# Two selective-scan layers: GpSimd's rows shifted by 8 bytes, side work moved to other steps, one logarithm for three units

## The chip, the cores and the metric

One Trainium2 chip, one of its cores. The metric is device time in microseconds for the whole program, one launch; the median of three runs of the kernel before is 16709.1 us (16696.06 to 16725.33). The engines are named by the profile's short names: PE (TensorE), DVE (VectorE), ACT (ScalarE), POOL (GpSimd), SP (SyncE).

## The reference

Four residual layers over x of shape (4, 96, 56, 56), each `x = x + L(groupnorm(x))`. Layer 0 is attention, layer 2 a local top-k attention with a feed-forward part; the change doesn't touch them. Layers 1 and 3 are state-space layers. Their scans, over 192 channels, 16 states and every position of the image in 8 (layer 1) or 4 (layer 3) orders, are what is changed.

Layer 1, per order:

```python
hc = hc * jnp.exp(d_t[..., None] * A[None]) + (d_t * u_t)[..., None] * B_t[:, :, None, :]
y_t = jnp.einsum('bkdn,bkn->bkd', hc, C_t)
```

Layer 3, per order:

```python
dlt = jax.nn.softplus(dlt)
phi = jnp.exp(-jnp.cumsum(dlt[..., None] * A_log[None, :, :, None, :], axis=3))
dbx = dlt[..., None] * jnp.swapaxes(b, 2, 3)[:, :, None] * xs[..., None]
h = phi * jnp.cumsum(dbx / (phi + 1e-12), axis=3)
y = jnp.einsum('bkdln,bknl->bkdl', h, c) + Ds[None, :, :, None]
```

In both, the step `dlt` is a softplus of a projection of the input, and B and C are rows of another projection of it.

## The kernel before, in words

`scans` handles one layer for one pair of images: two images of 192 channels make three blocks of 128 partitions, the **units** c = 0, 1, 2. It is called four times, twice with `ratio` false (layer 1) and twice with `ratio` true (layer 3). A **tile** q is 448 positions (T) of one order: 8 x 7 = 56 tiles a call in layer 1 (layer 1's image rows are 64 wide in memory, and half its orders are diagonals, whose pieces are cut in two), 4 x 7 = 28 in layer 3. A tile has 16 **groups**, one for each state n; the group's number over the whole call is g, r is its place in the tile, u = 3g + c counts group and unit. The **step** is s = 3r + c, 0 to 47 in a tile.

Main work of one group:
- ACT, `decay` (L1200): exp(dl x A) for each unit. Layer 1 has a ring of two in PSUM (NA = 2), so `decay(u)` waits for scan u - 2; layer 3 a ring of six in SBUF. In layer 3 ACT also does `weight` (L1210, a Tanh) into a ring of three in PSUM (NW = 3), where weight(u) waits for scan u - 3. `seed` (L1233) puts the start value at a row's head.
- POOL, `input1` (L1415): Tr = du x B for all three units at once, 128 x 1344, two groups ahead.
- DVE, `scan` (L1333), the recurrence over 449 elements (the start value and 448), one for each unit. Before it, in layer 3, `input2` (L1315) multiplies Tr with the weight. The state goes to PSUM for c < ON_DVE (two units in layer 1, one in layer 3) and else to `Hr` in SBUF.
- DVE `project` (L1340) and POOL `project` (L1424): Hc = state x C, the first for the states in PSUM and the second for those in `Hr` (one row of 448 in layer 1, two in layer 3). DVE does its projections between the scans of units 1 and 2.
- ACT, `keep_psum` (L1216) and `keep_sbuf` (L1221): the last column of each state into `st`, the start value for the next tile. A scan into PSUM waits for `st_done` of the group before, since it overwrites the state there.
- PE, `gather_n` (L1079): adds Hc into y in PSUM by a product with the identity.

Side work makes the next tile's `xs`, `dl`, `du` and (layer 3) `cs` while this tile runs, one tile ahead, at steps that tables fix (`SIDE`, `MERGE`, `AFTER`, and `prepare`/`prepare_late` of PE): ACT `gather` xs (L1114), PE `proj` (L1030), ACT `keep_dts` (L1126) and `keep_rows` (L1120), PE `pre_delta` (L1035), ACT `absolute` (L1133), `positive` (L1137), `expo` (L1142), in layer 1 `one_plus` and `minus_w`, ACT `loga` (L1158), PE `total` (L1043 to L1047, a sum by four products with the identity), ACT `delta` (L1162), then DVE `inputs` (L1283, du) in layer 1, and DVE `cumsum` (L1299) and POOL `inputs` (L1400, du) in layer 3. In layer 3 DVE `one_less` (L1290) makes w1. `merge` (L1191) writes the last tile's y back. In layer 3 the logarithm needs another table than Tanh and Exp, so that two table loads stand around it.

Every engine works its instructions in the order of the program; semaphores alone hold them. The loop of ACT, for each u: weight(u + 2) in layer 3, decay(u + 2), at c = 0 `seed`, at c = 2 `keep_sbuf`, then merge and side work of the step, and then at c = 1 `keep_psum`. `dl` and `du` have rows of 448 elements, `Hr` rows of 449, all packed without gaps.

## Time and profile before

| | us |
|---|---|
| median of 3 runs | 16709.1 |
| profiled execution, its own time | 16707.5 |
| its span | 16705.6 |
| DVE busy | 14926.7 (89%) |
| PE busy | 13571.3 (81%) |
| POOL busy | 12620.4 (76%) |
| ACT busy | 12298.3 (74%) |
| scans of layer 1, first call, 2350 to 6122 | 3771.1 |
| scans of layer 3, first call, 11001 to 13496 | 2494.4 |

A row of groups reads: line, engine, operation, tiles written and read with partitions x elements, count, then total busy us and mean ns of one, then the idle time just before them and what ended it. Times in windows and timelines are us from the span's start.

### The profile page before, as it was taken

Reading aid. Unit: us, or ns where it says so; the run is one execution under the profiler, and the core shown is the slowest. Engines: PE = TensorE matmul, PEld = TensorE weight load, DVE = VectorE, ACT = ScalarE, POOL = GpSimd, SP = SyncE. Lnnn points to the kernel's source line nnn. Section 1 sums busy time; section 2 is a strip of 40 time slices with the busy share of each in tenths; the row PEclk is TensorE's granted clock in tenths of the full one; section 3 lists DMA queues with packets and bytes.
Section 4 is the critical chain, followed back from the end, with each engine's and each line's share of the span. In section 5 each row is a group of like instructions: output and inputs, shape, how many; then the busy total and the mean of one; then the engine's idle time right before and its main releaser. Section 6 shows DMA issues by size and latency. Waiting matters only on the chain. (4 is left out here: it accounts for less than half of the span.)

```text
span 16705.6 us, 189354 instructions
## 1 busy us (share of the span) xinstructions
PE 13571.3 (81%) x38048; PEld 5620.9 (34%) x38048; DVE 14926.7 (89%) x20527; ACT 12298.3 (74%) x27189; POOL 12620.4 (76%) x6313
## 2 busy tenths in 40 slices
PE   7988978888888878888888886877777777777777
PEld 2222223333333333333333333533333333333333
DVE  6666669999999988999999996889999988999998
ACT  3555567777777766777777774588888968888996
POOL 0000059999999978999999994289999968999996
PEclk9999989999999999999999998988888888888988
DMA  1100023333333333333333332122222212222221
GB/s 24 19 14 17 5 74 113 112 113 112 111 111 111 111 96 107 112 113 113 111 111 111 111 111 80 49 78 85 85 84 83 84 48 80 85 85 84 83 84 46
DMA packets 543207, 1404.94 MB, mean 84 GB/s; under 512 B 135566, under 2 KB 191926, under 8 KB 539430
## 3 DMA queue, kind: packets, MB, share of 16 engines
q1 hardware_dynamic: 542034, 1392.84, 29.0%
q14 instruction: 868, 7.11, 0.2%
q8 instruction: 305, 5.00, 0.1%
HBM read 1311.24 MB, written 58.30 MB: 82 GB/s over the span
## 5 line engine op out<-in xcount | busy, mean ns | idle before, releaser
L1415 POOL TENSOR_TENSOR Tr<-du,BC 128x1344 f32<-128x1344 f32 x2688 | 8174.7, 3041 | 138.5 <-DVE du L1283 137.2
L1079 PE MATMUL PS<-Hc,ident 128*128 128x448 f32 x16128 | 7115.6, 578 | 1363.7 <-POOL Hc L1424 1133.9
L1079 PEld LDWEIGHTS PS<-Hc,ident 128*128 128x128 f32 x16128 | 3063.8, 199 | 5308.9 <-issue 2706.6
L1200 ACT ACTIVATE PS<-dl,A 128x448 f32<-128x448 f32 x5376 | 3401.9, 633 | 1599.8 <-DVE Hr L1333 1054.9
L1424 POOL TENSOR_TENSOR Hc<-Hr,BC 128x448 f32<-128x448 f32 (+1 forms) x2688 | 3603.9, 1341 | 602.2 <-DVE Hr L1333 527.1
L1333 DVE TENSOR_TENSOR_SCAN PS<-PS,Tr 128x449 f32<-128x449 f32 x3584 | 3711.0, 1078 | 93.0 <-ACT st L1216 82.4
L1340 DVE TENSOR_TENSOR Hc<-PS,BC 128x448 f32<-128x448 f32 x4480 | 2568.9, 607 | 0.0
L1210 ACT ACTIVATE PS<-cs,lneps,A 128x448 f32<-128x448 f32 x2688 | 1935.1, 720 | 18.8 <-DVE PS L1333 1.0
L1333 DVE TENSOR_TENSOR_SCAN Hr<-PS,Tr 128x449 f32<-128x449 f32 x1792 | 1938.4, 1082 | 0.0
L1333 DVE TENSOR_TENSOR_SCAN Hr<-Ar,PS 128x449 f32<-128x449 f32 x1792 | 1931.7, 1078 | 0.0
L1315 DVE SCALAR_TENSOR_TENSOR PS<-PS,Tr 128x448 f32<-128x448 f32 x2688 | 1651.1, 614 | 223.2 <-ACT PS L1210 203.6
L1200 ACT ACTIVATE Ar<-dl,A 128x448 f32<-128x448 f32 x2688 | 1765.8, 657 | 0.0
L486 DVE TENSOR_REDUCE mx<-PS 128x1 f32<-128x448 f32 (+1 forms) x2100 | 1207.9, 619 | 574.4 <-PE PS L276 559.2
L678 POOL MEMSET pad<- 128x348 f32 x6 | 2.3, 389 | 2217.9 <-POOLq L67 2217.9
L435 ACT ACTIVATE Pr<-PS 128x896 f32<-128x896 f32 (+1 forms) x1092 | 953.7, 887 | 668.3 <-PE PS L339 664.8
L1333 DVE TENSOR_TENSOR_SCAN PS<-Ar,PS 128x449 f32<-128x449 f32 x896 | 972.2, 1085 | 0.0
L1216 ACT ACTIVATE st<-PS 128x2 f32<-128x2 f32 (+1 forms) x2688 | 447.5, 166 | 637.9 <-DVE Hc L1340 635.5
L276 PE MATMUL PS<-K,Q 96*128 96x448 bf16 (+1 forms) x2100 | 800.3, 388 | 89.5 <-DVE mx L486 56.0
L1090 PE MATMUL PS<-yacc,ident 128*128 128x448 f32 (+15 forms) x1320 | 771.3, 693 | 84.8 <-ACT yacc L1191 82.1
L1035 PE MATMUL PS<-dts,dw 12*128 12x448 f32 x1008 | 522.9, 600 | 325.5 <-ACT dl L1137 203.8
L339 PE MATMUL PS<-Q,K 99*128 99x448 bf16 (+1 forms) x2100 | 748.9, 370 | 7.7 <-ACT Q L404 3.6
L1043 PE MATMUL PS<-du,ident 128*128 128x448 f32 x1008 | 517.4, 597 | 261.0 <-DVE cs L1299 177.2
(271 smaller groups left out, 15394.8 us busy)
## 6 DMA issues: line engine op xcount, KB each, us to landing
BC<-bcscratch SPq DMA_DIRECT2D x5376, 224.0 KB, 3.6
zscratch<-zst SPq DMA_DIRECT2D x84, 224.0 KB, 1.9
bcscratch<-rows SPq DMA_DIRECT2D x336, 56.0 KB, 1.7
z<-zscratch SPq DMA_DIRECT2D x28, 672.0 KB, 4.8
xg<-mid SPq DMA_DIRECT2D x12, 1176.0 KB, 7.9
xr<-mid SPq DMA_DIRECT2D x56, 168.0 KB, 2.7
rl<-rows SPq DMA_DIRECT2D x56, 168.0 KB, 3.3
Q<-part SPq DMA_DIRECT2D x72, 98.0 KB, 4.4
```

The source lines that it names most:

```text
L276: e.matmul(PS[0:qn, 5 + n % 2, 0:T], Q[s][0:96, q0:q0 + qn], KK[s][0:96, i * T:i * T + T], start=True, stop=True).then_inc(mx_mm, 1)
L435: e.activation(Pr[0:kn, n % NPR, 0:nt, :], PS[0:kn, 2 * (n % 2):2 * (n % 2) + nt, 0:T], ACT.Exp, scale=scale).then_inc(s_exp, 1)
L486: e.tensor_reduce(mx[0:qn, t, i:i + 1], PS[0:qn, 5 + n % 2, 0:T], AX.X, ALU.max).then_inc(mx_red, 1)
L1079: e.matmul(PS[:, YB + c, 0:T], K["ident"][:], Hc[:, g % NHC, c, :], start=False, stop=(nn == 15)).then_inc(y_done, 1)
L1090: e.matmul(view(PS[:, YB + c, :], ro, rd), K["ident"][:], view(yacc, c * n + off, dims), start=(i == 0), stop=False)
L1200: e.activation(decay_at(u, 1), dl[:, q % 2, c, :], ACT.Exp, scale=A[:, q // NT, c, nn:nn + 1]).then_inc(a_done, 1)
L1210: e.activation(PS[:, u % NW, 1:TW], cs[:, q % 2, c, :], ACT.Tanh, scale=A2[:, q // NT, c, nn:nn + 1], bias=K["lneps"][:]).then_inc(w_done, 1)
L1315: e.scalar_tensor_tensor(out=p, in0=p, scalar=1.0, in1=Tr[:, g % NTR, c, :], op0=ALU.add, op1=ALU.mult).then_inc(t2_done, 1)
L1333: e.tensor_tensor_scan(state_at(g, c, 0), decay_at(u, 0), input_at(g, c), 1.0 if ratio else 0.0, ALU.mult, ALU.add).then_inc(s_done, 1)
L1340: e.tensor_tensor(Hc[:, g % NHC, c, :], state_at(g, c, 1), BC[:, g % NBS, 1, :], ALU.mult).then_inc(h_done, 1)
L1415: e.tensor_tensor(Tr[:, g % NTR] if ratio else Tr[:, g % NTR, :, 1:TW], du[:, q % 2], b, ALU.mult).then_inc(t_done, 1)
L1424: e.tensor_tensor(Hc[:, g % NHC, ON_DVE:3], Hr[:, g % NH, :, 1:TW], c_, ALU.mult).then_inc(hp_done, 1)
```

## The change

Three things, all in `scans`.

1. `dl`, `du` and `Hr` get rows with a pitch of 452 elements (1808 bytes) and an offset of two elements, so that the rows that POOL reads, `dl` and `du` from their first element and `Hr` from its second, begin 8 bytes behind a multiple of 16. `BC`, `xs`, `Tr` and `Hc` stay as they are.
2. Steps of the side work move. Layer 3: third gather 8 to 10, dts and rows 10, 11 to 13, 14, the nine softplus steps from 13..23 to 16..28, logarithm 25 to 29, deltas 32, 36, 41 to 34, 38, 42, DVE's `one_less` 26 to 30, cumsums 33, 37, 42 to 35, 39, 43, PE's `proj`, `pre_delta` one group later, all three `total` behind `gather_n`. Layer 1: the third delta 41 to 40, and ACT's `keep_psum` goes ahead of merge and side work of its step. `total` takes `dl` and `du` first and waits for `minus` and `logd` only ahead of the products that need them.
3. In layer 3 one `Ln` over 128 x 1344 takes the place of three over 128 x 448.

```diff
-    TW = T + 1
+    TW, TP = T + 1, T + 4
...
-        xs, dl, du = sb("xs", [128, 3, T]), sb("dl", [128, 2, 3, T]), sb("du", [128, 2, 3, T])
+        xs = sb("xs", [128, 3, T])
+        dl, du = (sb(i, [128, 2, 3, TP])[:, :, :, 2:2 + T] for i in ("dl", "du"))
...
-        Hr = sb("Hr", [128, NH, 3 - ON_DVE, TW])
+        Hr = sb("Hr", [128, NH, 3 - ON_DVE, TP])[:, :, :, 1:1 + TW]
...
-                e.wait_ge(minus, q + 1 if ratio else 3 * q + c + 1)
                 if c and q:
                     e.wait_ge(total_read, 3 * q + c)
-                e.matmul(X_, K["ident"][:], du[:, s, c, :], start=True, stop=False)
+                e.wait_ge(expd, 3 * q + c + 1)
+                e.matmul(X_, K["ident"][:], dl[:, s, c, :], start=True, stop=False)
+                e.matmul(X_, K["ident"][:], du[:, s, c, :], start=False, stop=False)
+                e.wait_ge(minus, q + 1 if ratio else 3 * q + c + 1)
                 e.matmul(X_, K["nident" if ratio else "ident"][:], w1[:, c, :], start=False, stop=False)
                 e.wait_ge(logd, 3 * q + c + 1)
-                e.matmul(X_, K["ident"][:], logs(q)[:, c, :], start=False, stop=False)
-                e.matmul(X_, K["ident"][:], dl[:, s, c, :], start=False, stop=True).then_inc(x_full, 1)
+                e.matmul(X_, K["ident"][:], logs(q)[:, c, :], start=False, stop=True).then_inc(x_full, 1)
 
             def prepare(q, r):
-                if r == 3:
+                first = 4 if ratio else 3
+                if r == first:
                     proj(q)
-                elif r in (4, 5):
-                    pre_delta(q, r - 4)
+                elif r in (first + 1, first + 2):
+                    pre_delta(q, r - first - 1)
                 elif r == 6 and not ratio:
                     pre_delta(q, 2)
-                elif r == (10 if ratio else 9):
+                elif r == 9 and not ratio:
                     total(q, 0)
-                elif r == 11 and ratio:
-                    total(q, 1)
 
             def prepare_late(q, r):
-                if r == 6 and ratio:
+                if ratio and r == 7:
                     pre_delta(q, 2)
-                elif r == 10 and not ratio:
-                    total(q, 1)
-                elif r == 12:
-                    total(q, 2)
+                elif ratio and 10 <= r < 13:
+                    total(q, r - 10)
+                elif not ratio and r in (10, 12):
+                    total(q, r // 2 - 4)
...
             def logs_together(q, i):
-                for c in range(3):
-                    loga(q, c)
+                e.wait_ge(expd, 3 * q + 3)
+                if q:
+                    e.wait_ge(cs_ready, 3 * q)
+                e.activation(logs(q)[:], du[:, q % 2], ACT.Ln, bias=K["one"][:]).then_inc(logd, 3)
...
             if ratio:
-                SIDE = {gather: (5, 7, 8), rows_or_dts: (10, 11), absolute: (13, 17, 21), positive: (14, 18, 22),
-                        expo: (16, 20, 23), logs_together: (25,), delta: (32, 36, 41)}
+                SIDE = {gather: (5, 7, 10), rows_or_dts: (13, 14), absolute: (16, 20, 25), positive: (17, 22, 26),
+                        expo: (19, 23, 28), logs_together: (29,), delta: (34, 38, 42)}
             else:
                 SIDE = {gather: (4, 6, 7), rows_or_dts: (10, 11), absolute: (13, 16, 19), positive: (14, 17, 20),
                         expo: (15, 18, 21), one_plus: (22, 23, 25), minus_w: (24, 27, 30), loga: (26, 28, 31),
-                        delta: (29, 35, 41)}
+                        delta: (29, 35, 40)}
...
                 if c == 2:
                     keep_sbuf(g)
+                if c == 1 and not ratio:
+                    keep_psum(g)
                 if q and s in MERGE:
                     merge(q - 1, MERGE.index(s))
                 if q + 1 < NQS:
                     prepare(q + 1, s)
-                if c == 1:
+                if c == 1 and ratio:
                     keep_psum(g)
...
-                if ratio and s == 26:
+                if ratio and s == 30:
                     one_less(q)
...
-            AFTER = (33, 37, 42) if ratio else (31, 37, 42)
+            AFTER = (35, 39, 43) if ratio else (31, 37, 42)
```

## Rows read from the trace of the kernel before

**Rows 1.** The page: busy times; one group with what ended its idle time.

```profile
PE 13571.3 (81%) x38048; PEld 5620.9 (34%) x38048; DVE 14926.7 (89%) x20527; ACT 12298.3 (74%) x27189; POOL 12620.4 (76%) x6313
...
L1424 POOL TENSOR_TENSOR Hc<-Hr,BC 128x448 f32<-128x448 f32 (+1 forms) x2688 | 3603.9, 1341 | 602.2 <-DVE Hr L1333 527.1
```

**Rows 2.** Windows, first scan stage of each layer: length, busy by engine, clock, DMA.

```profile
core 0: us, PE busy (x) PEld busy (x) DVE busy (x) ACT busy (x) POOL busy (x), PEclk, DMA share, GB/s
2350.40:6121.50 3771.10, 3243.55 (x7832) 1402.07 (x7832) 3706.97 (x4635) 2833.68 (x7110) 3584.84 (x1786) 0.99 0.38 111
...
11001.00:13495.40 2494.40, 1848.26 (x3814) 768.01 (x3814) 2380.47 (x3231) 2221.20 (x4685) 2290.91 (x972) 0.89 0.29 83
```

**Rows 3.** DVE's waits, layer 1, 2350 to 6122: us, times, longest.

```profile
DVE PS L1333 <- ACT st L1216: 40.3, 112, 0.9
DVE du L1283 <- ACT dl L1162: 18.1, 55, 0.6
```

**Rows 4.** DVE's waits, layer 3, 11001 to 13496.

```profile
DVE PS L1315 <- ACT PS L1210: 101.6, 69, 2.7
```

**Rows 5.** Timelines of DVE and ACT, layer 1, a diagonal tile's steps 4 to 6.

```profile
5715.55 2.08 DVE L1333 TENSOR_TENSOR_SCAN PS<-PS,Tr 128x449 f32<-128x449 f32 x2 [0.38 <-ACT st L1216]
...
5714.26 1.10 ACT L1114 ACTIVATE xs<-xc 128x264 f32<-128x264 f32 x2
```

**Rows 6.** Timeline of POOL, layer 1, groups 3 and 4: start, us.

```profile
2357.05 1.13 POOL L1424 TENSOR_TENSOR Hc<-Hr,BC 128x448 f32<-128x448 f32 x1
...
2361.12 0.98 POOL L1424 TENSOR_TENSOR Hc<-Hr,BC 128x448 f32<-128x448 f32 x1
```

**Rows 7.** Groups by form, whole span.

```profile
L1415 POOL TENSOR_TENSOR Tr<-du,BC 128x1344 f32<-128x1344 f32 x2688 | 8174.7, 3041 | 138.5 <-DVE du L1283 137.2 <-PE PS L1079 1.1
...
L1400 POOL TENSOR_TENSOR du<-dl,xs 128x448 f32<-128x448 f32 x168 | 190.8, 1136 | 77.9 <-ACT dl L1162 73.1 <-PE PS L1079 4.8
...
L2377 ACT ACTIVATE E<-S,nb 112x616 f32<-112x616 f32 x40 | 32.3, 808 | 49.7 <-DVE nb L2502 49.7
...
L2377 ACT ACTIVATE E<-S,nb 112x315 f32<-112x315 f32 x16 | 8.9, 557 | 20.7 <-DVE nb L2502 20.5
```

**Rows 8.** Timeline of POOL, layer 3: L1424 during L1290, and the next.

```profile
11921.55 2.46 POOL L1424 TENSOR_TENSOR Hc<-Hr,BC 128x896 f32<-128x896 f32 x1 [0.42 <-DVE Hr L1333]
...
11930.16 1.92 POOL L1424 TENSOR_TENSOR Hc<-Hr,BC 128x896 f32<-128x896 f32 x1 [3.15 <-DVE Hr L1333]
```

**Rows 9.** Timelines of DVE and ACT, layer 1, a tile's steps 41 and 42.

```profile
3064.27 1.08 DVE L1333 TENSOR_TENSOR_SCAN Hr<-PS,Tr 128x449 f32<-128x449 f32 x1
...
3066.67 0.62 DVE L1283 TENSOR_TENSOR du<-PS,xs 128x448 f32<-128x448 f32 x1 [0.32 <-ACT dl L1162]
...
3065.45 0.64 ACT L1200 ACTIVATE PS<-dl,A 128x448 f32<-128x448 f32 x1 [0.89 <-DVE Hr L1333]
```

**Rows 10.** Timelines of DVE and ACT, layer 3, a tile's steps 25 to 28.

```profile
11921.39 0.83 DVE L1290 TENSOR_SCALAR w<-du 128x1344 f32<-128x1344 f32 x1
11924.91 0.63 DVE L1315 SCALAR_TENSOR_TENSOR PS<-PS,Tr 128x448 f32<-128x448 f32 x1 [2.68 <-ACT PS L1210]
...
11919.70 1.28 ACT L1158 ACT_TABLE_LOAD   x1
11920.99 1.79 ACT L1158 ACTIVATE cs<-du,one 128x448 f32<-128x448 f32 x3
```

**Rows 11.** Timelines of PE, ACT, DVE around step 10 in layer 3; one window there.

```profile
11979.51 4.17 PE L1030 MATMUL PS<-xs,xp 128*76 128x448 f32 x6 [1.97 <-ACT xs L1114]
...
11983.78 0.54 ACT L1126 ACTIVATE dts<-PS 12x448 f32<-12x448 f32 x1 [1.80 <-PE PS L1030]
...
11985.15 0.63 DVE L1315 SCALAR_TENSOR_TENSOR PS<-PS,Tr 128x448 f32<-128x448 f32 x1 [1.34 <-ACT PS L1210]
...
11980.00:11983.40 3.40, 3.40 (x6) 1.25 (x5) 3.40 (x6) 1.98 (x5) 3.40 (x2) 0.50 0.30 76
```

**Rows 12.** Timeline of PE, layer 3: first and last products of a sum.

```profile
11937.84 0.99 PE L1043 MATMUL PS<-du,ident 128*128 128x448 f32 x2 [2.37 <-DVE cs L1299]
...
11941.29 1.48 PE L1047 MATMUL PS<-dl,ident 128*128 128x448 f32 x2
```

More of the change, by code:

```diff
@@ L1155, in loga @@
                 e.wait_ge(expd, 3 * q + c + 1)
-                if ratio and q:
-                    e.wait_ge(cs_ready, 3 * q)
                 e.activation(logs(q)[:, c, :], du[:, q % 2, c, :], ACT.Ln, bias=K["one"][:]).then_inc(logd, 1)
@@ L1244, in act @@
                 positive(0, c)
-            for step in (expo, loga) if ratio else (expo, one_plus, minus_w, loga):
+            for step in (expo,) if ratio else (expo, one_plus, minus_w, loga):
                 for c in range(3):
                     step(0, c)
+            if ratio:
+                logs_together(0, 0)
             for c in range(3):
```

## The prediction

> **What bounds the kernel now.** I read four views in this order: busy times of the page, windows over the four scan stages, VectorE's own waits there, and the timeline around each wait.
>
> The page gives VectorE (DVE) 89% of the span, ScalarE (ACT) 74%, GpSimd (POOL) 76% [rows 1]. The change touches only the scans, and a stage of these takes 3771.1 us in layer 1 and 2494.4 us in layer 3 [rows 2]. Each layer has two such stages of one and the same code, for two pairs of images; I take the second as the first, 12.53 of 16.71 ms in all. In them VectorE is busy 98% (3706.97 of 3771.10) and 95% (2380.47 of 2494.40), GpSimd 95% and 92%. Both look like the bound, so the waits decide. In layer 1 VectorE waits for GpSimd in no row that is listed: 40.3 us in 112 waits for ScalarE's `st` (L1216), 18.1 us in 55 for its `dl` (L1162) [rows 3]. In layer 3 it waits 101.6 us in 69 waits for ScalarE's weights (L1210) [rows 4]. GpSimd in turn waits for VectorE: 527.1 us for L1333 ahead of its L1424 [rows 1]. So VectorE is the bound, with a few holes that ScalarE makes, and GpSimd follows it. VectorE's instructions overlap by about 0.09 us when nothing holds them (two scans of 1.08 take 2.08 together [rows 5]), so a hole costs its idle time plus 0.09.
>
> **Part 1: the starts of the rows.** In layer 1 GpSimd's L1424 takes 1.13 us for group 3 and 0.98 for group 4, and so on in threes: 1.13, 0.98, 0.98 [rows 6]. Its operand `Hr` has a pitch of 449 elements: its three slots begin 4, 8 and 12 bytes behind a multiple of 16 (the program places tiles at multiples of 32 bytes), and BC at 0. The long one is the first slot, so offsets 0 to 4 are slow and 8 to 12 fast. L1400, both operands at 0, takes 1136 ns: slow too [rows 7]. One row of 448 at 1131 and three at 3041 (L1415) give 955 per row and 176 fixed; the fast 978 gives 802 per row. In layer 3 L1424 reads a slow and a fast row: 176 + 955 + 802 = 1933, measured 1.92 where nothing disturbs it [rows 8]. The model holds, and behind the change every row lies at 8. L1415: 3041 to 176 + 3 x 802 = 2582, 2688 times, 1234 us. L1424: 0.15 on a third of 1792, 90 us; 0.153 on 896, 137 us. L1400: 0.153 x 168, 26 us. GpSimd loses 1487 us of work. On the path that is worth about nothing: no hole of VectorE ends with GpSimd. I take 3 us, for the first L1415s of each stage that VectorE has to await (two of them, 0.46 each, in four stages), and keep 0 to 10. ScalarE, VectorE and TensorE read and write these rows as well. No row has ScalarE read `dl` at 8 (L1200), and I take no difference (bounds -5 to +5 ns on 2 x 2688 + 2688 instructions beside slack, zero on the path).
>
> The Trainium skill (GPSIMD Engine Reference, Elementwise — side-by-side cycle accounting) calls about 2.6 cycles per element the floor of a two-input operation, whatever the start; by it the shift would bring GpSimd nothing. At the 1.2 GHz that the page gives, that is an estimated 2.17 ns per element; the fast rows run at 802/448 = 1.79 ns, so the trace speaks against it, and as GpSimd isn't the bound the time would be the same either way.
>
> **Part 2: layer 1, `keep_psum` ahead of the side work.** At steps s = 1, 4, 7 ScalarE first does a merge or a gather, then L1216, and the scan of the next group waits for `st`. One such hole is 0.38, behind a gather of 1.10 [rows 5]. Now L1216 goes first: it waits only for VectorE's second L1340, then takes 0.17, with a whole scan (1.0) of cover. Behind it on ScalarE wait the side work and the next decay L1200. That decay couldn't start before the following scan ends anyway (it starts 0.10 behind it [rows 9]); it is due 0.9 after that end and takes 0.64. From the second L1340's end, L1216 leaves at 0.3, side work of up to 0.98 (start to start) at 1.25, the decay may start at 1.1 and must start by 1.3: everything fits, except s = 7 on diagonal tiles, where the gather of s = 6 already ran late: there 0.16 is left over, on 28 of 56 tiles of a stage (4.5 us). The 112 holes cost 40.3 + 112 x 0.09 = 50.4 us a stage. **Delta** of the third unit moves from s = 41 to 40: L1283 now waits 0.32 for it [rows 9]; at 40 it starts behind L1216 with the sums of TensorE complete, and is done before it is due. 18.1 + 55 x 0.09 = 23.0 us. Layer 1: 2 x (50.4 + 23.0 - 4.5) = 138 us. If only the half came: 69; if no residue stayed: 147.
>
> **Part 3: layer 3.** Holes of a stage by step, from the timeline of VectorE (overlap included): 27 at the logarithms, 2.68 idle + 0.09 [rows 10], 75 us; 27 of 0.23 just ahead, 6; 13 at s = 11 and 12, 20; 14 at s = 9 of 0.65, 9; s = 3 and 6 on transposed tiles, 9. Together 119.
> *Logarithms.* Three L1158 take 1.79 us with two table loads of 1.28 around [rows 10]. One over 1344 columns: the slope from 315 to 616 columns is (808 - 557)/301 = 0.834 ns [rows 7], so 0.654 + 896 x 0.000834 = 1.40; 0.39 less. But it moves from s = 25 (c = 1) to 29 (c = 2), and so behind `keep_sbuf`, which waits for the scan of c = 2. Count from the start of the c = 1 scan: keep_sbuf ends at 3.44, load to 4.73, Ln to 6.14, load to 7.43, weight to 8.16; VectorE is due at 5.30 (scans, L1315, L1290). Hole 2.9, as now: 24.91 - 22.13 = 2.78. Gain of the shorter Ln: nothing. The 0.23 ahead goes, since ScalarE's side work there is no longer on four steps in a row (20 to 23). Together 81 to 77: 4 us.
> *L1290* reads `du`, now three rows with gaps. It takes 834 ns for 1344 elements, and while it runs GpSimd's L1424 took 2.46 for 1.92 [rows 8]. The Trainium skill (VectorE: DVE Perf Modes, Mode 2×_2P) asks that the outermost counts of source and destination be both even or odd and equal. By it, with `w` still one run of 1344 against three rows, the double rate is lost. Bounds from rows: 834 to 3 x 0.61 = 1830. Either way it lies within the 2.9 us in which VectorE awaits the weight: 0 on the path, and up to 1.0 x 54 = 54 us if that cover were gone. I keep 0.
> *Steps 11, 12.* L1126 waits 1.80 for the six L1030 records of 4.17 us, in a stretch with TensorE's granted clock at 0.50, its lower level of 1.2 GHz, behind a wait of its own of 1.97 us for the third gather at s = 8; VectorE then idles 1.34 [rows 11]. Now the third gather is at 10 and L1126 at 13, three steps for two: 1.7 us more room, more than the 1.34. 20 us go to 2.
> *Step 9.* The gather of s = 8 leaves: 9 to 2 us. Steps 3 and 6 stay.
> *What is late next:* cumsums at 35, 39, 43 and deltas at 34, 38, 42: the sum of the third unit has three steps for four. From cumsum to delta I count 5.2 us; the sum's eight records took 4.9 in a stretch where the clock fell to its lower level (records of 1.48 for two instead of 0.99) [rows 12]: it fits. GpSimd's L1400 waits a unit longer; it then has 2.6 + 1.8 + 1.0 us of work until the next tile's first product and 1.9 us in hand.
> Layer 3: 2 x (4 + 18 + 7) = 58; I take off 4 a stage for holes at the new places: 50 us.
>
> **Sum.** 16707.5 (the profiled execution; its span is 16705.6, the median 16709.1, so no correction) - 138 - 50 - 3 = 16516; forecast **16518 us**, 1.1% less.
>
> **Rivals.**
> *A. The logarithm brings its saving:* if ScalarE reached it as early as today, 0.39 x 54 = 21, and the new places cost nothing (8), no residue (9): 16480. For it: ScalarE has more idle steps ahead of s = 29. Against: keep_sbuf stands in front.
> *B. In layer 1 the wait moves to the decay.* Twelve of 16 c = 1 steps have side work, now all behind L1216. If the decay came 0.08 late on each: 12 x 0.08 x 112 = 108 us back: 16626. It decides from side work over 1.0 us, or if L1216 starts more than 0.1 behind L1340. For it: the margin at gathers is only 0.05 to 0.2; against: nine of the twelve are single instructions on 448 columns, of the kind of L1162 and L1158 (a third of 1.79 us [rows 10]), with half a us of room.
> *C. Slower: TensorE late at the end of layer 3's tiles.* The third sum starts behind the cumsum of s = 39 instead of 37. If TensorE then carries the backlog of L1079 over the tile's end at half clock, merges and L1340 (ring of three) wait. Two steps are 3.4 us; 54 x 3.4 = 184 plus layer 3's lost gain of 50: 16752. It decides once TensorE still has over two groups waiting at s = 45. Against: TensorE is busy 1848 of 2494 us [rows 2], so it has room, and GpSimd's product, which it waits for, comes earlier now.
> *D. GpSimd's saving reaches the end:* only if VectorE's holes were GpSimd's. Its ceiling is all holes but the logarithms': 147 + 88 + 3: 16470; joined with A's 21, 16449.
>
> **How the numbers follow.** Forecast (16490 to 16560) 62%; A and D together 14%; B, full or in part (16560 to 16640), 17%; C in full 3%; C in part, or an offset that makes ScalarE or VectorE slower (16640 to 16740) 4%. Range 16450 to 16640. About 0.2% (33 us) is what a measurement of this kernel tells from no change. Faster by more than that 0.93, within it 0.04, slower 0.03.
>
> **What would show it.** L1415 at 2.58 and L1424 at 0.98 in all slots and 1.78 in layer 3; no wait of VectorE for L1216 or L1162 in layer 1, its busy share there near 99.8%; scans of 3702 and 2470 us; the hole at the logarithms still 2.7 to 2.9, now behind L1290; no wait of L1126. Wrong it would be if L1200 appears among VectorE's waits, if L1333 or L1200 last longer, or if TensorE appears behind L1340.

## The result, and the profile after

The kernel after takes 16480.4 us (median of 4 runs, 16477.67 to 16489.0); the kernel before, measured beside it, 16712.8 us (4 runs, 16696.06 to 16725.33). The ratio is 0.9862 with a 95% interval of [0.9845, 0.988]: 232 us, 1.4% less. The forecast was 16518 us, 38 us above the result and within its range.

The profiled execution has a span of 16478.4 us, 227.2 less than the 16705.6 of before. First the page: busy time, share of the span and instructions of each engine.

```profile
PE 13585.7 (82%) x38048; PEld 5582.2 (34%) x38048; DVE 14909.9 (90%) x20527; ACT 12365.2 (75%) x27077; POOL 11077.5 (67%) x6313
```

GpSimd lost 1543 us of work, 9% of the span, and the span fell by 1.4%: most of GpSimd's saving went into its own waiting. Second, the windows over the first scan stage of each layer, which answer to [rows 2]. The windows of [rows 2] lie 11 us behind the scans that they are meant for: the first scan of layer 1 starts at 2339.3, that of layer 3 at 10990.0. The lengths are right; from first scan to last VectorE was busy 3710.22 us and GpSimd 3594.92 in layer 1, 2386.12 and 2299.88 in layer 3.

```profile
core 0: us, PE busy (x) PEld busy (x) DVE busy (x) ACT busy (x) POOL busy (x), PEclk, DMA share, GB/s
2342.00:6034.50 3692.50, 3247.99 (x7844) 1406.62 (x7844) 3691.01 (x4645) 2872.74 (x7120) 3135.26 (x1790) 0.99 0.40 113
10832.70:13294.00 2461.30, 1858.61 (x3820) 750.61 (x3821) 2397.43 (x3243) 2226.91 (x4648) 1990.04 (x975) 0.90 0.30 85
```

| scan stage, us | before | after | less | forecast |
|---|---|---|---|---|
| layer 1, first and second call | 3771.1, 3771.6 | 3692.5, 3695.4 | 154.8 | 138 |
| layer 3, first and second call | 2494.4, 2495.4 | 2461.3, 2460.3 | 68.2 | 50 |
| everything else | | | 4.2 | 3 |

The last row says nothing: outside the four stages the profiles of the kernels below differ by up to 39 us (4163 to 4202), where nothing was changed.

In layer 1 VectorE is now busy 3691.01 of 3692.50 us. Its waits there, against [rows 3]:

```profile
DVE PS L1338 <- POOL Tr L1420: 2.6, 1, 2.6
DVE PS L1338 <- ACT PS L1201: 0.6, 1, 0.6
```

Both old waits are gone, and the decay that now stands behind the side work (L1201) is waited for once, 0.6 us. In layer 3 the one wait that is listed is still that for the weight, against [rows 4]; behind it stands the timeline of VectorE and of ScalarE around the logarithm of one tile (start, us, instruction, and in brackets the idle time before it).

```profile
DVE PS L1320 <- ACT PS L1211: 62.5, 45, 2.1
```

```profile
11761.17 1.09 DVE L1338 TENSOR_TENSOR_SCAN PS<-Ar,PS 128x449 f32<-128x449 f32 x1
11762.17 1.54 DVE L1295 TENSOR_SCALAR w<-du 128x1344 f32<-128x1344 f32 x1
11765.79 0.63 DVE L1320 SCALAR_TENSOR_TENSOR PS<-PS,Tr 128x448 f32<-128x448 f32 x1 [2.08 <-ACT PS L1211]
```

```profile
11760.01 0.66 ACT L1201 ACTIVATE Ar<-dl,A 128x448 f32<-128x448 f32 x1
11760.77 0.21 ACT L1222 ACTIVATE st<-Hr 128x2 f32<-128x2 f32 x1
11761.00 1.28 ACT L1173 ACT_TABLE_LOAD   x1
11762.29 1.42 ACT L1173 ACTIVATE cs<-du,one 128x1344 f32<-128x1344 f32 x1
11763.73 1.28 ACT L1211 ACT_TABLE_LOAD   x1
11765.03 0.73 ACT L1211 ACTIVATE PS<-cs,lneps,A 128x448 f32<-128x448 f32 x1
```

The chain keep_sbuf, table, Ln, table, weight is the one of the forecast. The wait is shorter than the 2.68 us of [rows 10], but not since the weight comes earlier: `one_less` (L1295) now fills 1.54 us of it instead of 0.83. VectorE's hole, counted from the end of the scan ahead to the next `input2`, is about as long as it was: 3.53 us here, 3.43 by [rows 10] and the scan that ends at 11921.48 there.

GpSimd's groups by form (busy us, mean ns of one, idle time before it and what ended that), against [rows 1, 7, 8]:

```profile
L1420 POOL TENSOR_TENSOR Tr<-du,BC 128x1344 f32<-128x1344 f32 x2688 | 6895.0, 2565 | 97.0 <-DVE du L1288 94.2 <-issue 2.7
L1429 POOL TENSOR_TENSOR Hc<-Hr,BC 128x448 f32<-128x448 f32 x1792 | 1750.5, 977 | 1059.0 <-DVE Hr L1338 1059.0
L1429 POOL TENSOR_TENSOR Hc<-Hr,BC 128x896 f32<-128x896 f32 x896 | 1587.0, 1771 | 693.7 <-DVE Hr L1338 673.2 <-DMA BC<-bcscratch 19.8 <-PE PS L1080 0.8
```

2565 for 3041, 977 for 1030 and 1771 for 1962 ns. Ahead of L1429 GpSimd now waits 1732 us for VectorE's scan, where it waited 527: it has more slack than it had.

**Holes by step.** For layer 3 I add up, over the first call, the idle time of VectorE before each of its instructions, by the step whose scan it follows, each with the 0.09 us by which neighbours overlap; the number of holes is in brackets.

| step | before | after |
|---|---|---|
| 3, 6 | 2.8 (13), 6.3 (14) | 3.0 (13), 6.7 (14) |
| 9 | 9.1 (14) | 0 |
| 11, 12 | 17.2, 2.4 | 0 |
| 24 | 6.2 (27) | 0 |
| 26, now 30 | 74.8 (27) | 58.5 (27), and L1295 longer by 27 x 0.71 = 19.1 |
| all | 119.0 | 68.9 (88.0 with L1295) |

### The profile page after: what moved, and what is told of

Its sections match the earlier page's. It is cut to its first block and busy times, and to the rows that moved or that the text cites. A ratio compares the mean times of both kernels' runs of the same rounds, so it can differ in the third digit from the quotient of the medians.

```text
span 16478.4 us, 189136 instructions
## 1 busy us (share of the span) xinstructions
PE 13585.7 (82%) x38048; PEld 5582.2 (34%) x38048; DVE 14909.9 (90%) x20527; ACT 12365.2 (75%) x27077; POOL 11077.5 (67%) x6313
## 5 line engine op out<-in xcount | busy, mean ns | idle before, releaser
L1080 PE MATMUL PS<-Hc,ident 128*128 128x448 f32 x16128 | 7138.2, 577 | 1272.7 <-POOL Hc L1429 1060.2
L1420 POOL TENSOR_TENSOR Tr<-du,BC 128x1344 f32<-128x1344 f32 x2688 | 6895.0, 2565 | 97.0 <-DVE du L1288 94.2
L1080 PEld LDWEIGHTS PS<-Hc,ident 128*128 128x128 f32 x16128 | 3028.5, 198 | 5272.8 <-issue 2613.9
L1429 POOL TENSOR_TENSOR Hc<-Hr,BC 128x448 f32<-128x448 f32 (+1 forms) x2688 | 3337.5, 1242 | 1752.7 <-DVE Hr L1338 1732.2
L1201 ACT ACTIVATE PS<-dl,A 128x448 f32<-128x448 f32 x5376 | 3403.4, 633 | 1202.2 <-DVE Hr L1338 789.1
L1338 DVE TENSOR_TENSOR_SCAN Hr<-PS,Tr 128x449 f32<-128x449 f32 x1792 | 1931.0, 1078 | 0.0
L1201 ACT ACTIVATE Ar<-dl,A 128x448 f32<-128x448 f32 x2688 | 1764.7, 657 | 0.0
L1044 PE MATMUL PS<-dl,ident 128*128 128x448 f32 x1008 | 509.2, 588 | 236.8 <-issue 225.7
```

Source lines behind the costliest of these rows:

```text
L1080: e.matmul(PS[:, YB + c, 0:T], K["ident"][:], Hc[:, g % NHC, c, :], start=False, stop=(nn == 15)).then_inc(y_done, 1)
L1201: e.activation(decay_at(u, 1), dl[:, q % 2, c, :], ACT.Exp, scale=A[:, q // NT, c, nn:nn + 1]).then_inc(a_done, 1)
L1338: e.tensor_tensor_scan(state_at(g, c, 0), decay_at(u, 0), input_at(g, c), 1.0 if ratio else 0.0, ALU.mult, ALU.add).then_inc(s_done, 1)
L1420: e.tensor_tensor(Tr[:, g % NTR] if ratio else Tr[:, g % NTR, :, 1:TW], du[:, q % 2], b, ALU.mult).then_inc(t_done, 1)
L1429: e.tensor_tensor(Hc[:, g % NHC, ON_DVE:3], Hr[:, g % NH, :, 1:TW], c_, ALU.mult).then_inc(hp_done, 1)
```

## The experiments

**Do starts behind multiples of 16 bytes set GpSimd's speed, and which?** One stage of products on GpSimd alone, with all four layers left out (one run):

```diff
+    a, b, o = (
+        [chip.sb(ctx, p + n, [128, 3, 452]) for n in names] for p in ("a", "b", "o"))
...
+                            e.tensor_tensor(at(o[k], k, n), at(a[i], i, n), at(b[j], j, n), ALU.mult).then_inc(done, 1)
```

> Layers left out: the kernel copies x to the output and times GpSimd's products alone, 448 and 3 x 448 elements, first and second operand each starting 0, 4, 8 or 12 bytes behind a multiple of 16, output at 0 or 8. Theory 1 (what counts is the distance of the two operands' starts within 16 bytes): fast (about 0.98 and 2.57 us) where they differ by 8 or 12, slow (1.13 and 3.04) where by 0 or 4. Rival (what counts is the first operand's start alone): fast for the first at 8 or 12 whatever the second. The output's offset counts in neither.

A tile's name says by how many bytes (a for the first operand, b for the second, o for the output; nil, four, eight, twelve) it begins behind a multiple of 16. Groups by form, rows of 3 x 448:

```profile
L2721 POOL TENSOR_TENSOR onil<-aeight,bfour 128x1344 f32<-128x1344 f32 x4 | 12.1, 3018 | 0.3
L2721 POOL TENSOR_TENSOR oeight<-aeight,beight 128x1344 f32<-128x1344 f32 x4 | 12.1, 3018 | 0.3
L2721 POOL TENSOR_TENSOR onil<-anil,bnil 128x1344 f32<-128x1344 f32 x4 | 12.1, 3014 | 0.3
L2721 POOL TENSOR_TENSOR onil<-anil,beight 128x1344 f32<-128x1344 f32 x4 | 10.3, 2568 | 0.3
L2721 POOL TENSOR_TENSOR oeight<-aeight,bnil 128x1344 f32<-128x1344 f32 x4 | 10.3, 2568 | 0.3
L2721 POOL TENSOR_TENSOR onil<-afour,beight 128x1344 f32<-128x1344 f32 x4 | 10.3, 2563 | 0.3
```

All sixteen pairs of starts come out by one number, the first operand's start less the second's, modulo 16: at 0 or 4 a product takes 3014 to 3048 ns (1125 to 1131 for one row), at 8 or 12 it takes 2562 to 2568 (974 to 981). An output that begins at 8 instead of 0 changes nothing in the four pairs in which it was tried (starts of 0 and 8). Rows at 8 are fast because BC is at 0; with both at 8 the product is slow.

**What are the rows worth alone?** Only the shift, on the kernel before:

```diff
-    TW = T + 1
+    TW, TP = T + 1, T + 4
...
-        xs, dl, du = sb("xs", [128, 3, T]), sb("dl", [128, 2, 3, T]), sb("du", [128, 2, 3, T])
+        xs = sb("xs", [128, 3, T])
+        dl, du = (sb(i, [128, 2, 3, TP])[:, :, :, 2:2 + T] for i in ("dl", "du"))
...
-        Hr = sb("Hr", [128, NH, 3 - ON_DVE, TW])
+        Hr = sb("Hr", [128, NH, 3 - ON_DVE, TP])[:, :, :, 1:1 + TW]
```

> The kernel before with the pitch of 452 and the 8 bytes alone, every step where it was. GpSimd does about 1500 us less work (L1415 near 2.57 us, L1424 near 0.98 and 1.77). Theory 1 (VectorE is the bound and no hole of it is GpSimd's): -3 to -10 us against before, VectorE's waits for L1216 and L1162 in layer 1 and for L1210 in layer 3 unchanged within 10%, and GpSimd only waits longer for L1333. L1290 takes 1.54 instead of 0.83 us inside the hole at the logarithms, whose idle part falls from 2.68 to about 2.0. Rival (GpSimd's saving reaches the end, through TensorE and the merges): -30 us or more, and the waits of step 11 in layer 3 shrink.

16723.1 us against 16713.7, ratio 1.0006 [0.9996, 1.0016]: no change, where 3 to 10 us less were expected. GpSimd is as fast as in the kernel after (its line here, then the window of the first stage of layer 3):

```profile
L1416 POOL TENSOR_TENSOR Tr<-du,BC 128x1344 f32<-128x1344 f32 x2688 | 6895.0, 2565 | 148.4 <-DVE du L1284 148.3
```

```profile
10983.90:13483.20 2499.30, 1874.55 (x3822) 770.53 (x3822) 2405.89 (x3243) 2227.62 (x4702) 1993.37 (x975) 0.88 0.29 83
```

Some 1500 us of GpSimd's work gone, and nothing of the span. Layer 3 is even 5 us a call longer than in [rows 2]: the holes at steps 11 and 12 grew from 19.6 to 23.6. `one_less` has gone from 0.83 to 1.54 us, but that is hidden: the hole behind it shrank from 74.8 to 56.2 us a call, by 0.69 for each of 27.

**What is layer 1's order worth alone?** `keep_psum` first and the third delta at step 40, on the kernel before:

```diff
-                        delta: (29, 35, 41)}
+                        delta: (29, 35, 40)}
...
                 if c == 2:
                     keep_sbuf(g)
+                if c == 1 and not ratio:
+                    keep_psum(g)
...
-                if c == 1:
+                if c == 1 and ratio:
                     keep_psum(g)
```

> The kernel before with layer 1's two moves alone: keep_psum ahead of merge and side work, third delta at step 40. Theory 1 (the holes of layer 1 are all ScalarE's order): -150 us, 0.991 of before, each of layer 1's scan stages from 3771 to 3694 us, layer 3 untouched. Rival (a part of layer 1's gain came with GpSimd's shorter products): -100 us or less, and the rest of the waits named with GpSimd or TensorE.

16561.2 us, ratio 0.991 [0.9895, 0.9925], 152 us less. The window of the first stage of layer 1:

```profile
2341.90:6034.70 3692.80, 3247.28 (x7844) 1406.46 (x7844) 3691.14 (x4645) 2872.95 (x7120) 3590.67 (x1790) 0.99 0.38 113
```

Set beside the kernel after this is the clearest pair of the study: GpSimd is busy 3590.67 us here and 3135.26 there, and the stage lasts 3692.8 and 3692.5. All of layer 1's gain is the order of ScalarE's work.

**Are the rows worth nothing under the new order too?** The kernel after, with all rows at 4 bytes, where a product is slow. That is slower than the packed rows of the kernel before, of which some were fast; new steps with packed rows weren't run.

```diff
-        dl, du = (sb(i, [128, 2, 3, TP])[:, :, :, 2:2 + T] for i in ("dl", "du"))
+        dl, du = (sb(i, [128, 2, 3, TP])[:, :, :, 1:1 + T] for i in ("dl", "du"))
...
-        Hr = sb("Hr", [128, NH, 3 - ON_DVE, TP])[:, :, :, 1:1 + TW]
+        Hr = sb("Hr", [128, NH, 3 - ON_DVE, TP])[:, :, :, 0:TW]
```

> The changed kernel with the rows at 4 bytes behind a multiple of 16 instead of 8, pitch 452 kept. GpSimd is slow again in every row: L1420 3.04 us, L1429 1.13 and 2.09. Theory 1: at most 15 us slower than the changed kernel, so -215 us against before; GpSimd per group in layer 1 4.17 + gaps against a period of 4.12 for VectorE, so it just becomes the bound there if its two instructions leave more than 0.05 us between them: then up to 0.15 us a group, 1792 groups, 270 us back. Rival (offset is what gives the gain): slower than the changed kernel by 100 us or more.

16520.0 us, ratio 0.9884 [0.9869, 0.9899], 40 us above the kernel after (28 by the spans of the two profiles). Theory 1 had at most 15, its rival 100 or more: neither came. Layer 1 is the same (3695.7 and 3692.2 us), so that GpSimd doesn't become the bound there; layer 3 is longer by 15.2 and 16.1. GpSimd's larger product in layer 3 takes 2084 ns; with packed rows it took 1962, and in the kernel after it takes 1771:

```profile
L1429 POOL TENSOR_TENSOR Hc<-Hr,BC 128x896 f32<-128x896 f32 x896 | 1866.9, 2084 | 173.8 <-DVE Hr L1338 173.8
```

ScalarE's wait for `proj` in the first call of layer 3, here and in the kernel after:

```profile
ACT dts L1127 <- PE PS L1031: 18.6, 15, 1.9
```

```profile
ACT dts L1127 <- PE PS L1031: 1.0, 1, 1.0
```

VectorE has 12.5 to 14.8 us of new holes at steps 14 and 15, right behind. TensorE around `proj` in the third tile, here and in the kernel after:

```profile
11023.58 3.27 PE L1080 MATMUL PS<-Hc,ident 128*128 128x448 f32 x4 [2.51 <-POOL Hc L1429]
11026.69 2.42 PE L1031 MATMUL PS<-xs,xp 128*76 128x448 f32 x6
```

```profile
11024.96 3.14 PE L1080 MATMUL PS<-Hc,ident 128*128 128x448 f32 x4 [2.35 <-POOL Hc L1429]
11027.90 2.79 PE L1031 MATMUL PS<-xs,xp 128*76 128x448 f32 x6
```

In both TensorE waits for GpSimd's product, takes it (L1080) and then comes to `proj` (L1031). In the kernel after `proj` starts 1.4 us behind the gather of `xs` that it needs, with rows at 4 bytes 3.8 us. ScalarE's and VectorE's instructions on these rows last as long in both kernels, within 2 ns.

Lateness alone isn't enough, though. The granted clock in the 4 us ahead of `proj` was 0.57 to 0.72 in all eleven tiles of the first call whose `dts` waited over 1 us; where it was 1.0, `dts` waited 0.21 at most. The kernel after has such stretches too, and one listed wait. It takes both: GpSimd's product late, and TensorE at its lower level of 1.2 GHz for most of the time behind it. So GpSimd's speed does reach the end in layer 3, through TensorE, by some 15 us a call between all rows slow and all rows fast. What the shift gives against packed rows under the new steps stays open.

**Is the long logarithm worth its 0.37 us where it stood?** One Ln at step 25, on the kernel before:

```diff
-                for c in range(3):
-                    loga(q, c)
+                e.wait_ge(expd, 3 * q + 3)
+                if q:
+                    e.wait_ge(cs_ready, 3 * q)
+                e.activation(logs(q)[:], du[:, q % 2], ACT.Ln, bias=K["one"][:]).then_inc(logd, 3)
```

> The kernel before with one Ln over 128 x 1344 in the place of three, at the old step 25. Theory 1 (a logarithm that stays ahead of the engine's bookkeeping brings all it saves): 1.79 to 1.42 us for each of 54 holes, -20 us, the idle part of the hole from 2.68 to 2.31. Rival (the hole is set by the table loads, and the three were hidden in part): under -5 us.

16709.7 us against 16720.7, ratio 0.9991 [0.9982, 1.0]: 11 us less, half of what was expected and at the edge of no change. The waits of VectorE in the first call of layer 3, against [rows 4]:

```profile
DVE PS L1317 <- ACT PS L1212: 96.9, 75, 2.3
DVE cs L1301 <- ACT dl L1162: 1.4, 6, 0.3
```

The hole behind the logarithm shrank from 74.8 to 64.9 us a call, which is 0.37 for each of 27, as worked out. Most of it came back: the holes at steps 11 and 12 grew from 19.6 to about 26 us a call, in 20 tiles instead of 13, and 2 us a call are new at the second cumsum (the second row above). In these 20 tiles of the first call `proj` took 3.4 to 4.2 us at a granted clock of 0.59 to 0.70, in the other seven 2.48 at 1.0; the kernel before has the same two kinds. So the wait goes with TensorE's granted clock during `proj`. That a tile which is shorter by 0.37 us moves the stretches of lower clock is likely, but no run separates it.

**Does `keep_sbuf` cost the logarithm its saving?** In the kernel after, the logarithm ahead of it:

```diff
+                ahead = ratio and s in SIDE[logs_together] and q + 1 < NQS
+                if ahead:
+                    prepare(q + 1, s)
                 if c == 2:
                     keep_sbuf(g)
...
-                if q + 1 < NQS:
+                if q + 1 < NQS and not ahead:
```

> The changed kernel with the logarithm of step 29 ahead of keep_sbuf instead of behind it. Theory 1 (at 29 the logarithm awaits VectorE's scan through keep_sbuf, and this ate the saving of the single Ln): the block starts 0.39 us earlier, and keep_sbuf's 0.2 comes behind it; the hole's idle part 2.08 to about 1.87, -11 us against the changed kernel. Rival (the block's start doesn't matter, its length does): no change, within 3 us.

16471.1 us, ratio 0.9845 [0.983, 0.9859]: 9 us less than the kernel after, and its two stages of layer 3 are shorter by 5.3 us each; the hole goes from 58.5 to 52.8 us a call, 0.21 each. So yes, in part: counted from the start of VectorE's scan of c = 2, the first table load starts 0.31 us earlier, and the second 0.21, since `keep_sbuf` now stands between the `Ln` and it.

**What does the lost double rate of `one_less` cost?** The kernel after, with `w1` in rows of the same pitch as `du`:

```diff
-        w1 = sb("w1", [128, 3, T])
+        w1 = sb("w1", [128, 3, TP])[:, :, 2:2 + T]
```

> The changed kernel with w1 in rows of pitch 452 too, so that L1295 has three rows on both sides. By the Trainium skill (VectorE: DVE Perf Modes, Mode 2x_2P) the double rate comes back, since both outermost counts are 3: 1.54 to 0.83 us. Theory 1 (it lies in the hole at the logarithms): the hole's idle part grows by the same 0.71 us, and the time stays within 5 us of the changed kernel. Rival (L1295 is on the path): -38 us (54 x 0.71).

16479.1 us, ratio 0.9848 [0.9833, 0.9862]: the time of the kernel after. Whatever L1295 gains, the hole behind it grows by (58.5 to 63.0 us a call). But the rate didn't come back in full: L1295 takes 1370 instead of 1540 ns, where 830 were expected. The timelines of DVE and POOL at one logarithm:

```profile
11761.76 1.37 DVE L1295 TENSOR_SCALAR w<-du 128x1344 f32<-128x1344 f32 x1
```

```profile
11760.41 1.77 POOL L1429 TENSOR_TENSOR Hc<-Hr,BC 128x896 f32<-128x896 f32 x1 [0.78 <-DVE Hr L1338]
11762.14 2.95 POOL L1420 TENSOR_TENSOR Tr<-du,BC 128x1344 f32<-128x1344 f32 x1
```

L1295 starts 0.42 us before L1429 ends and takes about 1370 ns (1365 to 1374) in all 54 such places; in the two where GpSimd is idle it takes 1093. The L1420 that runs beside its rest takes 2.95 us instead of 2.56. In the kernel after neither is disturbed: L1295 takes 1534 to 1553 ns everywhere and L1420 2.56. So with equal rows on both sides the two engines get in each other's way, as GpSimd's L1424 was held up in [rows 8], and with unequal rows they don't. The Trainium skill (SBUF — State Buffer, Who interferes with whom) says that an operation of VectorE in the double-rate mode and one of GpSimd exclude each other for a whole instruction. The mutual delay agrees; its size doesn't quite: L1420 starts 0.99 us before L1295 ends and loses only 0.38, and L1295 loses 0.28 to the 0.42 of L1429.

**Can ScalarE be freed ahead of the logarithm?** A weight, a decay and `keep_sbuf` stand right ahead of the logarithm (the last two are in the timeline of ScalarE above, at 11760.01 and 11760.77). Here up to two decays are made in advance, the logarithm goes ahead of `keep_sbuf`, and `keep_sbuf` waits until behind the next weight:

```diff
-            made = 0
+            made, kept = 0, None
...
-                while made < min(u + 3, NU):
+                lead = (1 if 11 <= s < 18 else 2 if 18 <= s < 29 else 0) if ratio else 0
+                while made < min(u + 3 + lead, NU):
                     decay(made)
                     made += 1
                 if u < 0:
                     continue
+                if kept is not None:
+                    keep_sbuf(kept)
+                    kept = None
                 if c == 0 and g + 1 < NG:
                     seed(g + 1)
-                if c == 2:
+                if ratio and s in SIDE[logs_together] and q + 1 < NQS:
+                    kept = g
+                elif c == 2:
                     keep_sbuf(g)
```

> The changed kernel with ScalarE's decays of layer 3 one unit further ahead from step 11 and two from 18 (the ring of six holds them), none at steps 29 and 30, the logarithm ahead of keep_sbuf, and this behind the next weight. Theory 1 (the hole is the time from the last weight ahead of the logarithm to the first behind it, against a ring of three weights): the block starts 0.93 us earlier, the idle part of the hole falls from 2.08 to about 1.15, -50 us against the changed kernel, 16430. Rival (the ring of three weights or keep_psum at step 28 holds the start): -15 us or less.

16458.0 us, ratio 0.9837 [0.9821, 0.9854]: 22 us less than the kernel after, where 50 were expected. The hole behind the logarithm alone gives 49 (58.5 to 34.2 us, twice), as worked out. VectorE's timeline there and three steps behind step 18:

```profile
11765.94 0.63 DVE L1326 SCALAR_TENSOR_TENSOR PS<-PS,Tr 128x448 f32<-128x448 f32 x1 [1.18 <-ACT PS L1211]
```

```profile
11748.00 0.63 DVE L1326 SCALAR_TENSOR_TENSOR PS<-PS,Tr 128x448 f32<-128x448 f32 x1 [0.20 <-ACT PS L1211]
```

The decay that is made ahead at step 18 comes back as a hole at step 21, in all 27 tiles: 7.7 us a call. That leaves 16.6 of 24.3, and the stages are shorter by 15.3 and 14.3 us.

**Is there a better place for them?** Two schedules. In the first (`early_lead`) the decays are made ahead at steps 8 and 11; in the second (`all`) at 9 and 12, and the merges and gathers of layer 3 stand at every other step. The edits are shown against the version with decays ahead.

```diff
-                lead = (1 if 11 <= s < 18 else 2 if 18 <= s < 29 else 0) if ratio else 0
+                lead = (1 if 8 <= s < 11 else 2 if 11 <= s < 29 else 0) if ratio else 0
```

> The version with decays ahead (16458.0 us), with the same merges and gathers as the kernel after, and the two extra decays at steps 8 and 11 instead of 11 and 18. Theory (the hole at step 21 comes from the extra decay at 18, inside the stretch of steps 13 to 28 in which ScalarE is busy all the time): the hole at step 21, 7.7 us a call, goes, the one at 30 stays at 34 and those at 3 and 6 stay: 15 us less, 16443 us. Rival (ScalarE is as full from step 5 to 12 as from 13 to 28): the hole only moves to a step from 9 to 15 and the time is 16458 us, as it was.

```diff
-                SIDE = {gather: (5, 7, 10), rows_or_dts: (13, 14), absolute: (16, 20, 25), positive: (17, 22, 26),
+                SIDE = {gather: (6, 8, 10), rows_or_dts: (13, 14), absolute: (16, 20, 25), positive: (17, 22, 26),
...
-            MERGE = (1, 2, 4) if ratio else (0, 1, 3)
+            MERGE = (0, 2, 4) if ratio else (0, 1, 3)
...
-                lead = (1 if 11 <= s < 18 else 2 if 18 <= s < 29 else 0) if ratio else 0
+                lead = (1 if 9 <= s < 12 else 2 if 12 <= s < 29 else 0) if ratio else 0
```

> The kernel after, with the two decays ahead put where ScalarE has idle time (one at step 9, one at step 12, kept to step 28) instead of at steps 11 and 18, and in layer 3 the merges at steps 0, 2, 4 and the gathers at 6, 8, 10, so that no two of them stand in neighbouring steps. In the version with decays ahead (16458.0 us) the holes of layer 3 are, a call: step 3 2.8, step 6 6.7, step 21 7.7, step 30 34.2 us. Theory (a hole comes wherever ScalarE has more work than the scans leave it before the next weight; spreading removes it without another): the holes at 3, 6 and 21 go, 17.2 us a call, two calls, 34 less: 16424 us, range 16415 to 16440; step 30 stays at 34. Rival (between steps 8 and 14 ScalarE has no more than 0.1 to 0.3 us left a step, so the early decays and the gathers at 8 and 10 together are late): 3 and 6 go, 21 goes, but a new hole of 0.3 us a tile stands at a step from 11 to 15, 8 us a call: 16440 us.

16444.6 us for the first (ratio 0.9837 [0.9823, 0.9852], four runs from 16442.7 to 16448.5), 16472.9 for the second (0.9852 [0.9835, 0.9868]), beside the kernel before at 16717.1; the version with decays ahead stood beside it at 16720.7. Holes of VectorE in the first call of layer 3, us, worked out as above:

| kernel | 3 | 6 | 9 | 11, 12 | 14, 15 | 21 | 30 | all |
|---|---|---|---|---|---|---|---|---|
| after | 3.0 | 6.7 | 0 | 0 | 0.3 | 0 | 58.5 | 68.9 |
| decays ahead | 2.8 | 6.7 | 0 | 0 | 0 | 7.7 | 34.2 | 51.6 |
| early lead | 2.9 | 6.7 | 3.8 | 4.0 | 0 | 0 | 34.1 | 51.8 |
| all | 3.0 | 0 | 5.8 | 6.6 | 7.8 | 0 | 34.1 | 57.8 |

In their holes both go as the rivals have it: the holes moved, and their sum stayed or grew. In the second the hole at step 3 stayed, which theory and rival both had going, and the new ones are more than the rival's 8 us; its time is above even the rival's 16440. The first one's is the theory's (16443), but not by its reason, as the row of its holes shows. The new holes at steps 9 and 12 of the first, and at 9 and 11 of the second, are in 14 tiles of 28, those from tile 13 on, which is the first that gathers for a transposed order. There ScalarE's gathers and merges take about twice as long; groups by form in two short windows of the kernel after, first a tile of the plain orders, then one of the transposed:

```profile
L1115 ACT ACTIVATE xs<-xc 128x448 f32<-128x448 f32 x3 | 1.7, 561 | 0.0
L1192 ACT ACTIVATE yacc<-PS 128x448 f32<-128x448 f32 x3 | 1.6, 522 | 0.0
```

```profile
L1115 ACT ACTIVATE xs<-xc 128x448 f32<-128x448 f32 x3 | 3.1, 1039 | 0.1
L1192 ACT ACTIVATE yacc<-PS 128x448 f32<-128x448 f32 x3 | 3.1, 1019 | 0.0
```

That is 3 us more of ScalarE's work before step 11, so that in half of the tiles the early steps have no room for the decays of these two schedules. A second decay at step 18 has room in no tile (7.7 us at step 21, in all 27). The early lead's 13 us below the version with decays ahead aren't from these holes, and aren't shown to be a gain: both have a ratio of 0.9837 to the kernel before, the two stages of layer 3 differ by 0.7 and 1.3 us, and 5.6 us lie in layer 1, where nothing was changed. Its 16444.6 us is the lowest time of the study, 36 us below the kernel after; of these about 32 are in the stages of layer 3.

## Why the prediction was right, point by point

**GpSimd's work** was forecast at 1487 us less and fell by 1543. L1420 was put at 2582 and took 2565 ns, L1429 at 0.98 and 1.78 and took 0.977 and 1.771, L1405 978 against 983. It fell by more in L1420 (1280 us for 1234) and in layer 3's L1429 (171 for 137, since its two rows had cost 1962 ns and not 1933). The model of rows (a part for the instruction, a slow or a fast rate a row) holds. What it took for a property of a row's own start is one of the difference of two starts; here it came to the same, since BC is at 0. The figure of about 2.6 cycles in the Trainium skill (GPSIMD Engine Reference, Elementwise — side-by-side cycle accounting), an estimated 2.17 ns an element, fits the slow rows, 955/448 = 2.13 ns, and isn't a floor here: the fast rows run at 802/448 = 1.79 ns.

**That it would be worth about nothing** (3 us, 0 to 10) was right for layer 1 and for the rows alone (1.0006). It isn't right as a part of this change: between rows at 4 and rows at 8 lie 28 to 40 us, all in layer 3. The weak step is "no hole of VectorE ends with GpSimd". It held for the kernel before, even at one remove: there `proj` starts 0.05 us behind the gather of `xs` in all 27 tiles of the first call, behind 1.9 to 3.1 us of idle TensorE, as [rows 11] shows for one. It doesn't carry over to the new steps, where `proj` stands behind TensorE's gather of GpSimd's product, and I didn't follow that path. I gave the whole gain at steps 11 and 12 to the new steps; how much of it packed rows would have left is open, since that kernel wasn't run. That the sum still fits is luck in this part: it had a term for those holes, whichever edit closed them. Rival D, GpSimd's saving at the end, holds to this extent, though not by its condition.

**Layer 1**: 154.8 us for 138. With a hole counted as its idle time and 0.09, the timeline had 78.2 us a call before and has 4.6 now; the prediction took 50.4 + 23.0 = 73.4 from the list of waits and left 4.5. The residue was right as a whole (2.7 us on the diagonal tiles at step 10, the rest single ones). Two terms were short: 4.8 us a call of holes that the two rows of [rows 3] don't hold, and 3 to 5 us because scans right behind a hole last 1101 ns and others 1075, and the next instruction starts as much later. The first stage's groups: the kernel before, the one with layer 1's order alone, and the kernel after:

```profile
L1333 DVE TENSOR_TENSOR_SCAN PS<-PS,Tr 128x449 f32<-128x449 f32 x1792 | 1855.8, 1078 | 45.8 <-ACT st L1216 40.3 <-POOL Tr L1415 3.0
```

```profile
L1335 DVE TENSOR_TENSOR_SCAN PS<-PS,Tr 128x449 f32<-128x449 f32 x1792 | 1854.6, 1076 | 4.6 <-POOL Tr L1417 3.0 <-ACT PS L1200 0.4
```

```profile
L1338 DVE TENSOR_TENSOR_SCAN PS<-PS,Tr 128x449 f32<-128x449 f32 x1792 | 1851.2, 1073 | 4.0 <-POOL Tr L1420 2.6 <-ACT PS L1201 0.6
```

The holes account for the step from 1078 to 1076. The further 3 ns are undisturbed scans, 1072 in the kernel after for 1076; they bring nothing, since the next instruction starts no earlier and the stage lasts 3692.8 and 3692.5 us.

Rival B, the wait that moves to the decay, didn't come: 0.6 us in one wait.

**Layer 3**: 68.2 us for 50. The logarithm's gain was put at 4 us a call, and is 6.2 + 74.8 - 58.5 - 19.1 = 3.4. Step 9 gave 9.1 for 7, steps 11 and 12 gave 19.3 for 18, steps 3 and 6 stayed. The 4 us a call that I took off for holes at new places weren't needed (0.3 at step 14). So the gap is residues that I charged and that didn't come, 2.1 + 1.3 + 4, less 0.6 of the logarithm and 0.6 by which steps 3 and 6 grew. Of the 3 us a call that are left, somewhat over 1 is that VectorE's instruction behind a hole lasts longer here too (L1315 633 ns for 612, 121 times before and 57 after); the rest is open. The hole from keep_sbuf to weight, put at 2.9 us, is 2.08 + 0.09 + the 0.71 that `one_less` got longer, so its working was right. `one_less` came out at 1540 ns between the bounds of 834 and 1830, hidden as forecast.

**The rivals.** A (the logarithm keeps its saving) has the measured time, 16480, but fell in its mechanism: the hole at the logarithm is no shorter than before. Where `keep_sbuf` didn't stand in front, the hole did shrink, by the full 0.37 us at step 25 and by 0.21 at step 29. C (TensorE late at a tile's end) didn't appear: TensorE is in no listed wait of VectorE in the stages.

## What to carry to other kernels

Read who ends the bound engine's waits, not who is busiest: 455 us of GpSimd's work a stage were worth 0.3 us, and one small copy put ahead of the side work, with a step moved by one, 78. Then ask what the releaser itself waits for, one engine further back, and ask it of the new order, not of the old one; that is where GpSimd's speed did count. And once ScalarE has no idle time ahead of a bottleneck, moving its work only moves the hole: count its work between two such points, for the heaviest kind of tile, before moving anything.

## What the runs showed of the hardware

- GpSimd's product of two fp32 operands in SBUF depends on the first start less the second modulo 16 bytes: 0 or 4, 1125 to 1131 ns for 448 elements and 3014 to 3048 for 1344; 8 or 12, 974 to 981 and 2562 to 2568. An output at 8 instead of 0 made no difference.
- VectorE's one-source operation over 1344 elements took, with GpSimd idle, 860 ns from one run of elements to one, 1553 from three rows with gaps to one run, and 1093 from three such rows to three. 1093 lies a third of the way from 860 to 1553, as long as an operation would take that doubles the rate for two rows and not for the third (an estimate from these three times); no run tests that.
- In the kernel before, layer 1's scan of 449 elements into PSUM lasts 1101 ns where it follows a wait and 1075 where it doesn't, and what comes next starts 24 to 25 ns later.
- Under the old steps `proj`'s six records took 2.48 us at a granted clock of 1.0 and 3.4 to 4.8 where it was 0.50 to 0.70.
- One Ln over 1344 columns took 1419 ns, three over 448 took 1.79 us; the two table loads around it are 1.28 us each either way. The hole behind the three is still 58.5 of the 68.9 us that VectorE idles in a call of layer 3.
